# Head pairs written out instead of looped, and the es transposes moved into the slot scores' bank

## What is computed

```python
s = hs @ Ws1.T @ Ws2.T + bs2                         # 64 slots per head
s = jnp.clip(s, -CLAMP, CLAMP)
z = jax.lax.cumlogsumexp(s, axis=2)
es = jnp.exp(s); enz = jnp.exp(-z)
A = jnp.where(mask, jnp.einsum('bhtd,bhjd->bhtj', q, k) * scale, 0.0)
ok = enz * jnp.einsum('bhtj,bhjm->bhtm', A, es)
qv = jax.nn.softmax(ok, axis=-1)
W2 = jnp.where(mask, jnp.einsum('bhtm,bhjm->bhtj', qv * enz, es), 0.0)
o = jnp.einsum('bhtj,bhjd->bhtd', W2, v)             # then a norm, a gate and Wo
```

## Time and profile before

| | us |
|---|---|
| median of three runs | 1188.34 |
| lowest and highest | 1185.62 and 1189.64 |
| profiled execution, its time | 1186.13 |
| profiled execution, span from first to last instruction | 1184.4 |
| TensorE busy | 1114.7 (94%) |
| VectorE busy | 943.1 (80%) |
| ScalarE busy | 642.1 (54%) |
| GpSimd busy | 419.6 (35%) |

### The profile page before, as it was taken

The page is one execution under the profiler, slowest core; times in us unless marked ns, Lnnn a source line. Parts: engine busy times, 40 slices in busy tenths (PEclk is TensorE's granted clock), DMA queues, the critical chain, the costliest instruction groups (busy, mean ns, idle before and its releaser), DMA issues.

```text
span 1184.4 us, 20879 instructions
## 1 busy us (share of the span) xinstructions
PE 1114.7 (94%) x6872; PEld 941.6 (79%) x6872; DVE 943.1 (80%) x1808; ACT 642.1 (54%) x1748; POOL 419.6 (35%) x306
## 2 busy tenths in 40 slices
PE   6789999999999998999989999899998999999995
PEld 5568888888788887888878888788887888788884
DVE  6888887888868887888877888778886888877763
ACT  5355564655645565555655556464563565655451
POOL 5233242433513335232443324343251433523231
PEclk9899999999999999999999999999999999999998
DMA  4001000100001000010000100001000100000001
GB/s 157 1 1 74 1 1 1 52 22 1 1 2 73 1 1 2 1 73 1 1 3 1 74 1 1 3 16 59 1 1 2 73 1 1 1 2 19 1 19 36
DMA packets 9117, 23.19 MB, mean 20 GB/s; under 512 B 816, under 2 KB 5808, under 8 KB 7984
## 3 DMA queue, kind: packets, MB, share of 16 engines
q1 hardware_dynamic: 9008, 21.76, 5.0%
HBM read 19.66 MB, written 2.10 MB: 18 GB/s over the span
## 4 chain that ended last, share of the span: by engine, by line
PE 71%; issue 8%; DVE 6%; ACT 6%; POOL 3%; POOLq 0%; DVEq 0%; ACTq 0%
PE bank L203 17%; PE bank L205 16%; PE bank L204 16%; PE bank L292 5%; ACT xs L568 3%; PE bank L305 3%; PE bank L349 2%; DVE xs L860 2%; POOL qkT L1087 2%; PE bank L294 2%; DVE Wt L740 2%; ACT xs L567 2%; PE bank L282 1%; PE bank L338 1%; PE bank L341 1%
## 5 line engine op out<-in xcount | busy, mean ns | idle before, releaser
L1096 POOL TENSOR_TENSOR inter_lo<-ffb,inter_hi 128x512 fp32r<-128x512 f32 x64 | 83.3, 1323 | 433.2 <-ACT inter_hi L617 433.2
L1087 POOL TENSOR_TENSOR qkT<-ra,xs 128x512 f32<-128x512 f32 x128 | 163.5, 1277 | 95.1 <-DVE xs L860 67.6
L586 ACT ACTIVATE sm<-bank,mx 128x64 f32<-128x64 f32 x256 | 76.3, 325 | 168.5 <-DVE mx L816 168.5
L857 DVE TENSOR_TENSOR ra<-bank,rope 128x512 f32<-128x512 f32 x128 | 88.0, 687 | 55.1 <-ACT xs L568 54.9
L805 DVE RECIPROCAL enzT<-enzT 128x256 f32<-128x256 f32 x64 | 111.6, 1744 | 0.0
L860 DVE TENSOR_TENSOR xs<-xs,rope 128x512 f32<-128x512 f32 x128 | 109.0, 852 | 0.0
L203 PE MATMUL bank<-xh,wqk_hi 128*128 128x512 f32 x256 | 107.4, 420 | 0.0
L203 PE MATMUL bank<-xh,wgu_hi 128*128 128x512 f32 x256 | 106.9, 418 | 0.0
L591 ACT ACTIVATE At<-bank 128x128 f32<-128x128 f32 x128 | 35.4, 276 | 132.0 <-DVE At L740 132.0
L205 PE MATMUL bank<-xh,wgu_lo 128*128 128x512 f32 x256 | 101.6, 397 | 0.0
L203 PE MATMUL bank<-wvg_hi,xh 128*128 128x512 f32 x256 | 101.4, 396 | 0.0
(11 more groups left out here) (137 smaller groups left out, 3211.5 us busy)
## 6 DMA issues: line engine op xcount, KB each, us to landing
raw<-in_w_qkvg SPq DMA_DIRECT2D x8, 1024.0 KB, 4.9
scaled<-in_w_scaled SPq DMA_DIRECT2D x8, 640.0 KB, 7.7
packed<-in_w_packed SPq DMA_DIRECT2D x8, 384.0 KB, 5.4
acc<-in_x SPq DMA_DIRECT2D x4, 512.0 KB, 8.6
out<-acc SPq DMA_DIRECT2D x4, 512.0 KB, 3.0
ws_raw<-in_w_slot SPq DMA_DIRECT2D x8, 48.0 KB, 1.8
rope<-in_rope_tab SPq DMA_DIRECT2D x1, 256.0 KB, 7.0
osq<-in_w_slot SPq DMA_DIRECT2D x1, 128.0 KB, 3.3
```

What stands on the lines that cost most here:

```text
L857: dve.tensor_tensor(two(ra[i % 2][:, :]), two(pj[i][:, :]), cos, ALU.mult).then_inc(cos_done, 1)
L1087: pool.tensor_tensor(qkT[:, i, :], ra[i % 2][:, :], xs[i % 2][:, :], ALU.add).then_inc(roped, 1)
L1096: pool.tensor_tensor(inter[1][e][:, :], ffb[e][:, :], inter[0][e][:, :].bitcast(F32), ALU.subtract).then_inc(inter_lo, 1)
```

## The change

The engine loops go: `each_stage` and SyncE's loop become Python loops, so all eight head pairs are straight code, and every wait compares with a constant. `sc_bank` goes too, and the roles are fixed: A and W by head or batch into bank 0 or 1, the slot scores S and the transposes E into bank 0, K into bank 1.

With that, E moves on TensorE from step 9 to behind half 1 of `outputs` in step 6, ahead of `project_vg` 3, and waits for es_ready alone. `copy_J` moves on ScalarE from between the two `square_o` to ahead of `softmax_exp`. A0 and A1 of the next stage then wait for W_off 4 * st - 1 and 4 * st, and no longer for J_ready; `slot_weights` 0 waits for J_ready instead of A_off and clip_done.

```diff
-SC_SLOTS = {"A": (0, 1, 2, 3), "S": (4,), "K": (5,), "W": (6, 7, 8, 9), "E": (10,)}
-SC_STEP = 11
...
-        def sc_bank(bp, kind, i=0):
-            return sc[(SC_STEP * bp + SC_SLOTS[kind][i]) % 2]
...
-            for bp in range(BP):
-                stage(0, bp, bp == 0, False)
-            with eng.Fori(1, HP - 1) as hp:
+            for hp in range(HP):
                 for bp in range(BP):
-                    stage(hp, bp, False, False)
-            for bp in range(BP):
-                stage(HP - 1, bp, False, bp == BP - 1)
+                    stage(hp, bp, hp == bp == 0, hp == HP - 1 and bp == BP - 1)
...
-            with sp.Fori(0, HP - 1) as hp:
+            for hp in range(HP - 1):
...
                 for i in (0, 1):
-                    if first and i == 1:
-                        pe.wait_ge(clip_done, 1)
-                    elif first or i == 1:
-                        pe.wait_ge(J_ready, st + 1)
+                    if first:
+                        pe.wait_ge(clip_done if i == 1 else J_ready, 1)
                     else:
-                        pe.wait_ge(W_off, 4 * st)
+                        pe.wait_ge(W_off, 4 * st - 1 + i)
                     scores(st, bp, i, hp)
...
-                slot_rows(st, bp)
+                slot_rows(st)
                 if not first:
                     outputs(st, 1, php, st + 1)
+                if not last:
+                    pe.wait_ge(es_ready, st + 2)
+                    slot_transpose(sc[0], esT[nbp % 2])
                 if not last:
                     project_vg(st + 1, nbp, nhp, 3, True)
                 pe.wait_ge(p_ready, st + 1)
...
                 pe.wait_ge(qe_ready, st + 1)
-                pe.wait_ge(A_off, 4 * st + 4)
-                if not last:
-                    pe.wait_ge(clip_done, st + 2)
+                if not last:
+                    pe.wait_ge(J_ready, st + 2)
                 slot_weights(st, bp, 0)
...
                 values(st, bp, 0)
-                if not last:
-                    pe.wait_ge(es_ready, st + 2)
-                    pe.wait_ge(W_off, 4 * st + 3)
-                    slot_transpose(sc_bank(bp, "E", 0), esT[nbp % 2])
...
-                softmax_exp(st, bp)
+                if not last:
+                    copy_J(st + 1, sc[0][:, :])
+                softmax_exp(st)
...
                 square_o(st, 0)
-                if not last:
-                    copy_J(st + 1, sc_bank(bp, "E", 0)[:, :])
                 square_o(st, 1)
```

More of the change, by code:

```diff
@@ L276, in slot_scores @@
                     pe.wait_ge(ws2_lo, 4 * hp + 4)
-                pe.matmul(sc_bank((bp - 1) % BP, "S")[:, :] if n is not None else sc[1][:, :],
+                pe.matmul(sc[0][:, :] if n is not None else sc[1][:, :],
                           ws2[:, :], h1[:, bp, :], start=True, stop=True).then_inc(S_full, 1)
@@ L289, in scores @@
                     pe.wait_ge(roped, 4 * st + 2 * h + 2)
-                dst = sc_bank(bp, "A", i)
+                dst = sc[b]
                 t0 = b * T
@@ L309, in slot_reads, with slot_rows @@
                 mm.then_inc(ok_full, 1)
-            def slot_rows(st, bp):
+            def slot_rows(st):
                 pe.wait_ge(okz_done, st + 1)
-                dst = sc_bank(bp, "K")
+                dst = sc[1]
                 for i in range(NT):
@@ L321, in slot_weights @@
                 t0 = b * T
-                pair = [(sc_bank(bp, "W", 2 * b + h), slice(h * M, (h + 1) * M)) for h in range(2)]
+                pair = [(sc[h], slice(h * M, (h + 1) * M)) for h in range(2)]
                 for dst, g in pair:
@@ L577, in copy_J, with softmax_exp @@
                 act.activation(esJ[:, :, :].rearrange("p n m -> p (n m)"), src, ACT.Copy).then_inc(J_ready, 1)
-            def softmax_exp(st, bp):
+            def softmax_exp(st):
                 act.wait_ge(mx_done, st + 1)
@@ L582, in softmax_exp @@
                 wait(act, rs_done, st)
-                src = sc_bank(bp, "K")
+                src = sc[1]
                 for g in range(8):
@@ L587, in softmax_exp, with off_diagonal @@
                 ins.then_inc(p_ready, 1)
-            def off_diagonal(diag, done, dst, bp, kind, st, i, scale):
+            def off_diagonal(diag, done, dst, st, i, scale):
                 act.wait_ge(diag, 4 * st + i + 1)
-                act.activation(dst[i][:, 1, :], sc_bank(bp, kind, i)[:, P:2 * P], ACT.Copy,
+                act.activation(dst[i][:, 1, :], sc[i % 2][:, P:2 * P], ACT.Copy,
                                scale=scale).then_inc(done, 1)
@@ L662, in stage @@
                 npar = (bp + 1) % 2
-                a_args = (A_diag, A_off, At, bp, "A", st)
-                w_args = (W_diag, W_off, Wt, bp, "W", st)
-                more = not (isinstance(hp, int) and hp == HP - 1)
+                a_args = (A_diag, A_off, At, st)
+                w_args = (W_diag, W_off, Wt, st)
+                more = hp < HP - 1
                 off_diagonal(*a_args, 0, SCALE)
@@ L734, in two, with diagonal @@
                 return ap.rearrange("p (b t) -> p b t", b=2)
-            def diagonal(full, done, dst, bp, kind, st, i, mask, used):
+            def diagonal(full, done, dst, st, i, mask, used):
                 dve.wait_ge(full, 4 * st + i + 1)
                 wait(dve, *used)
-                src = sc_bank(bp, kind, i)[:, 0:3 * P].rearrange("p (n t) -> p n t", n=3)
+                src = sc[i % 2][:, 0:3 * P].rearrange("p (n t) -> p n t", n=3)
                 dve.tensor_tensor(dst[i][:, 0:3:2, :], src[:, 0:3:2, :], mask[:, :, :], ALU.mult).then_inc(done, 1)
@@ L811, in softmax_in, with softmax_max @@
                 dve.tensor_tensor(okz[:, :], rg[0][:, :], enzT[par][:, :], ALU.mult).then_inc(okz_done, 1)
[L813 removed]
+            def softmax_max(st):
                 dve.wait_ge(K_full, st + 1)
                 wait(dve, p_ready, st)
[L816 removed]
+                dve.tensor_reduce(mx[:, :], sc[1][:, :].rearrange("p (g m) -> p g m", m=M),
                                   AX_X, ALU.max, negate=True).then_inc(mx_done, 1)
@@ L946, in stage @@
                 par, npar, pbp = bp % 2, (bp + 1) % 2, (bp - 1) % BP
-                more = not (isinstance(hp, int) and hp == HP - 1)
-                a_args = (A_full, A_diag, At, bp, "A", st)
-                w_args = (W_full, W_diag, Wt, bp, "W", st)
+                more = hp < HP - 1
+                a_args = (A_full, A_diag, At, st)
+                w_args = (W_full, W_diag, Wt, st)
                 if bp == 3 and more:
@@ L977, in stage @@
                 if not last:
-                    clip(st + 1, npar, sc_bank(bp, "S")[:, :])
+                    clip(st + 1, npar, sc[0][:, :])
                 if not first:
@@ L993, in stage @@
                     invert(st + 1, npar, 0)
-                softmax_max(st, bp)
+                softmax_max(st)
                 if not first:
```

## The result

The changed kernel takes 1241.17 us (median of four, 1240.6 to 1241.6) against 1186.98 us before: 1.045 times as long, 95% interval 1.043 to 1.048. The forecast was 1247 us, range 1224 to 1272, slower. Its profiled execution has a span of 1238.9 us against 1184.4, 54.5 us more.

The account below looks back on a forecast made before the run. TensorE, busy 94% of the span, was taken to bound the kernel. 1186.1 - 13.0 (loops) + 70.3 (stages) - 0.3 (stage 0) + 2.4 (clock) = 1245.5 us profiled, 1247 as median; range 1224 to 1272.

Parts of the forecast that it names:

- The copy ahead of the softmax decides: ScalarE, each stage: `copy_J` waits for E behind 24 matmuls of `outputs`, so the softmax starts 3.13 us later.
- the faster case: ScalarE: the copy fills idle time ahead of `mx`, so only the loops' 13 us count, 1175 us; chance 0.04.
- Size of pT's wait: TensorE ahead of pT, stages 1 to 30: it stands still for 1.9 us a stage.
- The stages: Tails of stages 1 to 30: later W copies add 2.20 to 2.65 us each, 70.3 us; stage 0 gives -0.3.
- the decode of about 1.2 us: VectorE in bp 1: queued behind `slot_query`, it moves the first `rope_cos` by 2.95 us and the stage grows 2.65 us.
- The loops: TensorE's branches: 9.7 us of issue gaps and 3.3 us of low clock behind two of them go, 13.0 us gained.
- The clock in the tails: bp 3 tails: the longer wait brings the clock down in half of seven cases, not two, adding 2.4 us.
- Oscillating clock: Rival: TensorE drops to 1.2 GHz after each of 30 waits at pT, 49 us more, 1296 us; chance 0.10.
- The absorbing tail: Rival: W copies do not move with the softmax, so a late TensorE finds them done, 1226 us; chance 0.05.
- Stalls of written-out code: Rival: straight code stalls where the loop did or elsewhere, the 13 us are not gained, 1260 us; chance 0.04.

Follow-up runs that it names:

- E halfway: The changed kernel with the transposes E moved forward, behind 12 of the 24 matmuls of `outputs` 1: 1203.1 us, 1.013 of the kernel before.
- the double copy: The changed kernel with a second, idle copy of 0.60 us on ScalarE ahead of the softmax: 1285.0 us, 1.083 of the kernel before.
- filling the remaining gap: The kernel before with loops written out and GpSimd's split of gate and up weights moved behind `rotate` 2: 1160.9 us, 0.978 of before.

## Why the prediction was right, step by step

- **The copy ahead of the softmax decides: right, and shown.** Its three supports were each tested: behind the softmax (57.8 us back), E halfway (1.43 us earlier, 1.42 us less wait), E behind K (1183.1 us). The point at which the faster case was to be decided, a copy that is over when the maxima are, held too: with E right behind K the softmax starts 0.2 us late, and the slowdown is gone.
- **Size of pT's wait: 1.9 us forecast, 1.66 measured.** Most of that is in how the two are counted: 1.9 is from start to start (671.13 - 669.24), 1.66 from the modelled end of the matmul before. From start to start pT could have come 0.23 us behind the last matmul of `project_vg` 3, at 698.41, and came at 700.23, 1.82 us later. The rest is the copy, which holds ScalarE for 0.50 us before the softmax starts, not 0.58. pT is 2.27 us behind its old distance to the maxima, not 2.36 (700.23 - 693.93 = 6.30 us, against 4.03 in the earlier trace rows).
- **The stages: +70.0 us forecast (70.3 - 0.3), 67.1 measured** without falls of the clock. bp 0 and bp 2 were right (2.20 forecast, 2.05 to 2.16 measured). bp 1 was too high: 2.65 forecast, 36.46 - 34.30 = 2.16 measured. The step that failed is the decode of about 1.2 us queued behind `slot_query`: its median is 1225 ns in the kernel before and 642 in after. The decode of stage 17 and GpSimd's first `hidden_lo` beside it, before and after:

```profile
670.23 1.30 POOL L1096 TENSOR_TENSOR inter_lo<-ffb,inter_hi 128x512 fp32r<-128x512 f32 x1 [14.82 <-ACT inter_hi L617]
670.72 1.23 DVE L867 TENSOR_SCALAR packed<-packed 128x768 int32<-128x768 int32 x1
```

```profile
701.87 1.30 POOL L1083 TENSOR_TENSOR inter_lo<-ffb,inter_hi 128x512 fp32r<-128x512 f32 x1 [17.17 <-ACT inter_hi L604]
702.94 0.64 DVE L854 TENSOR_SCALAR packed<-packed 128x768 int32<-128x768 int32 x1
```

  In both it ends 0.42 us after that GpSimd instruction, though it starts 0.49 us into it before and 1.07 us in after. The same holds for the kernel with the copy behind the softmax: 0.72 us in, 1.00 us long, end 0.41 us after. So its length is the time to GpSimd's end and a fixed rest; the forecast moved it and kept its length. No run was made for this.
- **The loops: -13.0 us forecast.** The two traces give -13.8: from pT to pT, the five stretches with a branch together shrank by 2.6 us, while the two like them without a branch grew by 2.25 and 2.22, which makes 11.2 for five. So the term is right for this change, in part by luck. What it left out shows in the kernel with only the loops written out, which gained 7.2 us: with the branch gone, the wait ahead of E stayed, and the clock fell behind it seven times instead of twice. The price of the loops by themselves, 14.4 us, shows only where that wait is gone too.
- **The clock in the tails: +2.4 us forecast, 0 measured.** The wait is 2.38 us ahead of `values` 1 in place of 2.5, and the clock fell two times in seven, as before. That it stayed at two is luck: over the other kernels with a tail wait of 2.0 to 2.7 us it fell three, three, five, six, seven and seven times in seven. More low clock came in the last stage.
- **The start: not forecast, +2.3 us.** pT of stage 0 is at 65.70 us instead of 63.38.
- **The sum.** From pT of stage 0 to that of stage 31 the trace has 50.3 us more: 64.1 for the stages and -13.8 for the loops; with 2.3 at the start and 1.8 behind pT of stage 31, that is the 54.5 between the spans. The forecast's 59.4 was 5 us above, by errors that partly cancel: 5.9 too much in the stages, 2.4 in the clock and 0.8 in the loops, and 4.1 at the two ends that it did not have.
- **The rivals.** Oscillating clock: not in after's 30 waits of 1.66 us, but half a microsecond away, as the double copy showed. That it stayed away is not shown by the earlier trace rows, on which the chance of 0.10 rested. The same gap ahead of pT of stage 0 brought the clock down at once in the written-out kernel:

```profile
65.54 0.66 PE L471 MATMUL bank<-ident,sm 128*128 128x128 f32 x4 [2.56 <-ACT sm L582]
...
67.00:70.00 3.00, 3.00 (x9) 2.23 (x7) 2.49 (x11) 1.80 (x4) 0.39 (x1) 0.50 0.02 5
```

  So it did, within 1.5 us behind the start of pT, in 8 of the 13 traces, that of after among them (a gap of 2.12 us). What a gap ahead of pT between 1.66 and 2.12 us does, no run shows. The absorbing tail: no; the W copies moved with the softmax. Stalls of written-out code: no issue wait of TensorE ahead of the scores in any written-out trace. On the branches the Trainium skill, page "Runtime: NRT & Kernel Launch", section "Instruction fetch mechanics", says that fetching ahead is sequential and a taken branch out of reach stalls for a fetch; the traces agree, with 0.8 us at one of the five branches of TensorE, 2.0 to 2.5 us at the other four, and nothing at the exit. That the stall is a fetch no run here shows.

## What to carry to other kernels

Where an engine works through its instructions in the order written, ask of every instruction that is moved what it waits for and who queues behind it: here a 0.6 us copy, placed ahead of the softmax, brought its producer's lateness into the path of the busiest engine, 60 us in all. Place it where its producer is already done, or put the producer forward with it.
When a gap of a busy TensorE is removed or grown, look at the granted clock behind the gaps that remain, and count in how many repeats it falls, since a gain can be handed back there; filling the remaining gap paid 19 us here, more than the loops did.
A duration of VectorE beside GpSimd holds for that neighbourhood only: 0.68 or 2.47 us, 1.23 or 0.64, 1.78 or 3.93 for the same instructions here.

## What the runs showed of the hardware that I had not expected

- TensorE's clock behind a gap ahead of pT, with long matmuls on both sides: no fall in 30 gaps of 1.65 to 1.66 us (in each of three traces), 15 in 30 at 2.15 us. Behind the wait of 2.0 to 2.1 us in the tail, with short matmuls around it, 2 in 7 in one kernel and 7 in 7 in another whose stream there is the same. Each costs 1.4 to 1.7 us.
- The written-out kernel without other changes spreads over 10 us between executions (1174.0 to 1184.1), the one whose tails have no such gap over 2.4 us (1159.9 to 1162.4). The granted clock goes with it, 0.985 in the fast executions and 0.976 to 0.981 in the slow ones. The gap alone does not make a spread: the kernel with the copy behind the softmax waits 2.27 us in the same tails and spreads over 2.2 us in ten executions.
- The same four VectorE instructions took 1.78 or 3.8 to 3.9 us. Without loops they start 0.3 to 1.0 us later and GpSimd's split 0.8 to 1.6 us earlier than with them, and so the two meet.
